# ScalarE as a second row fetcher in two attention stages, and the linear part of an elu on VectorE

## The reference

```python
x = x + gnn(layernorm(x), edges)
x = x + ffn(layernorm(x))

# gnn: one GCN layer (64 wide), two attention layers (4 heads of 64)
h = relu(segment_sum(h[src] * norm[:, None], dst, n) + b)      # GCN, then batch norm
# an attention layer
h = (x @ W).reshape(n, 4, 64)
e = leaky_relu(alpha_s[src] + alpha_d[dst])                    # one logit per edge and head
w = exp(e - emax[dst])
out = segment_sum((w / wsum[dst])[:, :, None] * h[src], dst, n) + b
h = elu(batch_norm(out))
```

## Time and profile before

| | |
|---|---|
| median of three runs | 8129.97 us |
| the profiled execution | 8128.7 us, its span 8126.9 us |
| busy over the span | PE 4740 us (58%), VectorE 4679 (58%), ScalarE 1679 (21%), GpSimd 5035 (62%) |
| GCN edge stage | about 355 to 2375 us |
| attention edge stages | about 2476 to 4557 and 4754 to 6831 us |
| input of the second attention layer | 4557 to 4750 us, its elu 4631 to 4733 |
| the expert part and the rest | 6831 us to the end |

### The profile page before, as it was taken

One profiled execution on the slowest core, in us unless ns is written; L12 is line 12 of the kernel. 1 busy time (PEld: TensorE's weight loads), 2 busy tenths in 40 slices (PEclk: granted clock), 3 DMA queues, 4 the chain that ended last, 5 costly groups with the idle time before them and its releaser, 6 DMA issues. The chain is left out here.

```text
span 8126.9 us, 152076 instructions
## 1 busy us (share of the span) xinstructions
PE 4740.2 (58%) x25092; PEld 3771.0 (46%) x25110; DVE 4678.9 (58%) x11632; ACT 1678.8 (21%) x7056; POOL 5035.3 (62%) x5320
## 2 busy tenths in 40 slices
PE   3444444444454666666656756565665556779994
PEld 3433333333343444444444544444444444559993
DVE  7722222222237777777777767777677777764445
ACT  3400000000022111111111431111111112563331
POOL 0177777777755777777777247777777774015552
PEclk9999999999997777877777787778787876869997
DMA  5411111111124555555555245555555553412226
GB/s 203 162 29 29 29 29 29 29 29 29 29 56 132 137 137 137 137 137 138 136 134 139 69 121 138 137 137 137 137 137 138 137 137 85 140 51 70 70 70 219
DMA packets 527200, 848.14 MB, mean 104 GB/s; under 512 B 147632, under 2 KB 373137, under 8 KB 519791
## 3 DMA queue, kind: packets, MB, share of 16 engines
q0 software_dynamic: 228576, 543.07, 26.7%
q1 hardware_dynamic: 265512, 274.99, 11.7%
q10 hardware_dynamic: 32358, 23.60, 0.9%
HBM read 750.78 MB, written 82.11 MB: 102 GB/s over the span
## 5 line engine op out<-in xcount | busy, mean ns | idle before, releaser
L769 POOL DMA_INDIRECT gat_rows<-gat_table,gat_idx x3278 | 3103.4, 947 | 1057.8 <-issue 944.7
L890 PE MATMUL gat_ps_sum<-gat_msg,gat_hot 128*128 128x260 f32 x6656 | 2267.8, 500 | 1263.5 <-DVE feat L909 1261.0
L890 PEld LDWEIGHTS gat_ps_sum<-gat_msg,gat_hot 128*128 128x128 f32 x6656 | 1562.4, 246 | 1605.0 <-DVE gat_msg L945 1150.5
L769 POOL DMA_INDIRECT gcn_rows<-gcn_table,gcn_idx x1614 | 1523.0, 944 | 787.4 <-issue 478.3
L890 PE MATMUL gcn_ps_sum<-gcn_rows,gcn_hot 128*128 128x64 f32 x3328 | 814.1, 426 | 1228.2 <-DMA gcn_rows<-gcn_table,gcn_idx 724.7
L890 PEld LDWEIGHTS gcn_ps_sum<-gcn_rows,gcn_hot 128*128 128x128 f32 x3328 | 741.1, 328 | 1301.2 <-DMA gcn_rows<-gcn_table,gcn_idx 658.3
L909 DVE SCALAR_TENSOR_TENSOR feat<-gcn_ps_sum,in_first,feat 128x64 f32 x416 | 118.0, 284 | 1572.2 <-PE gcn_ps_sum L890 1572.2
L873 PEld LDWEIGHTS gat_ps_near<-gat_tab,gat_hot_t 128*128 128x128 bf16 x6656 | 268.3, 101 | 766.4 <-issue 579.2
L945 DVE TENSOR_TENSOR gat_msg<-gat_rows,gat_ps_as 128x1024 f32<-128x1024 f32 x416 | 503.2, 1210 | 118.1 <-issue 117.4
L921 DVE TENSOR_TENSOR gat_hot<-gat_count,mod_t 128x512 f32<-128x512 f32 x832 | 566.4, 681 | 2.7
L873 PE MATMUL gat_ps_near<-gat_tab,gat_hot_t 128*128 128x24 bf16 x6656 | 309.8, 178 | 435.4 <-DVE gat_hot L921 431.3
(11 more groups left out here) (308 smaller groups left out, 6375.5 us busy)
## 6 DMA issues: line engine op xcount, KB each, us to landing
gat_mod<-mod_rows SPq DMA_DIRECT2D x832, 128.0 KB
gat_ahead<-gat_table SPq DMA_DIRECT2D x6400, 1.0 KB
gi_mods<-mod_rows SPq DMA_DIRECT2D x52, 1024.0 KB, 4.7
gat_rows<-gat_table,gat_idx POOLq DMA_INDIRECT x3278
gcn_ahead<-gcn_table SPq DMA_DIRECT2D x3200, 0.2 KB
gcn_ahead<-gcn_table ACTq DMA_DIRECT2D x3200, 0.2 KB
gcn_rows<-gcn_table,gcn_idx POOLq DMA_INDIRECT x1614, 2.4
gat_table<-feat SPq DMA_DIRECT2D x28, 910.0 KB, 5.3
```

What stands on the lines that cost most here:

```text
L769: pool.indirect_dma_start(B["rows"][:, j, k, :], None, table, bass.IndirectOffsetOnAxis(ap=B["idx"][:, j, k:k + 1], axis=0)).then_inc(rows ...
L890: mm = pe.matmul(B["ps_sum"][b][:, 0:width], B["hot"][:, j, k, :], rhs, start=(k == 0), stop=(k == CH - 1))
```

## The change

- The helpers of each kind of stage are listed as (period, first group): `HELPERS = {False: ((16, 2), (16, 9)), True: ((16, 2), (16, 9))}`. Attention stages (`True`) thus get the helper on ScalarE that the GCN stage has. GpSimd issues three gathers instead of four for the groups 25, 41, ... to 409, 25 groups per stage.
- ScalarE's program in an attention stage becomes push, weigh, stage, bring, fetch, with a loop of 32 turns instead of 16. Its push comes four turns ahead of the group that it serves (`lead` 4), in the GCN stage one.
- `landed` and `ahead` count for any period; consumers of a chunk wait for `pushed` of the helper that brought it.
- `pace` gets `spare`: the loop stops earlier, so that more of the last turns are unrolled. SyncE's and ScalarE's helper programs use it.
- In the elu, `straight` on ScalarE is removed and VectorE's `line` makes y into the same buffer, one block ahead of `clip` and `unite`.

```diff
-AHEAD = 16
-ATS = (2, 9)
-BURST = P // AHEAD
+HELPERS = {False: ((16, 2), (16, 9)), True: ((16, 2), (16, 9))}
...
-def pace(eng, n, steps, ring=2):
+def pace(eng, n, steps, ring=2, spare=0):
...
-    last = (n - max(leads)) // ring
+    last = (n - max(leads) - spare) // ring
...
-    helpers = 1 if gat else 2
+    helpers = len(HELPERS[gat])
...
-    def ahead(i, c):
+    def ahead(turn, i, c):
 
-        if isinstance(i, int) and AHEAD * i + c < AHEAD:
-            return []
-        return [h for h, at in enumerate(ats) if c % AHEAD == at]
+        return [(h, 16 * (turn // period) * i + 16 * ((c - at) // period)) for h, (period, at) in enumerate(helpers)
+                if c % period == at and not (isinstance(i, int) and turn * i + c < period)]
...
-            for k in range(CH - len(ahead(i, c))):
+            for k in range(CH - len(ahead(TURN, i, c))):
...
-    def helper(eng, h):
+    def helper(eng, h, lead=1):
...
-            if c % AHEAD == at - 1 and known(n):
+            if c % period == at - lead and known(n):
...
-        if gat:
-            pace(act, NG, [(weigh, 2), (stage, RING + 2)], AHEAD)
-        else:
-            bring, fetch, push = helper(act, 1)
-            pace(act, NG, [(push, -AHEAD), (stage, RING), (bring, AHEAD), (fetch, 0)], 2 * AHEAD)
+        bring, fetch, push = helper(act, 1, 4 if gat else 1)
+        steps = [(weigh, 2), (stage, RING + 2)] if gat else [(stage, RING)]
+        pace(act, NG, [(push, -period)] + steps + [(bring, period), (fetch, 0)], turn,
+             period + helpers[1][1])
...
                 def line(q):
-                    if q >= SLOTS:
+                    to = shf if elu else stage
+                    if elu:
+                        wait(dve, staged, q - (SLOTS - 1))
+                    elif q >= SLOTS:
                         dve.wait_ge(product, last(q - SLOTS))
                     for k in range(KP):
-                        ins = dve.tensor_scalar(some(stage, q, k), feat[0:KF, four(q), k * P:(k + 1) * P],
+                        ins = dve.tensor_scalar(some(to, q, k), feat[0:KF, four(q), k * P:(k + 1) * P],
                                                 scale[0:KF, k:k + 1], shift[0:KF, k:k + 1], ALU.mult, ALU.add)
                     ins.then_inc(shifted, 1)
...
-                turns(NQ, [(clip, 0), (unite, 0)] if elu else [(line, 0)])
+                turns(NQ, [(clip, 0), (line, 1), (unite, 0)] if elu else [(line, 0)])
...
-                def straight(q):
-                    wait(act, staged, q - (SLOTS - 1))
-                    for k in range(KP):
-                        ins = act.activation(some(shf, q, k), feat[:, four(q), k * P:(k + 1) * P], ACT.Identity,
-                                             scale=scale[:, k:k + 1], bias=shift[:, k:k + 1])
-                    ins.then_inc(shifted, 1)
...
-                turns(NQ, ([(expo, 2), (straight, 2)] if elu else []) + [(place, 0)])
+                turns(NQ, ([(expo, 2)] if elu else []) + [(place, 0)])
```

More of the change, by code:

```diff
@@ L741, in fast_edges, with landed @@
     rows_used = msg_made if gat else summed
[L742 to L754, removed]
-    def ahead(i, c):
-        if isinstance(i, int) and AHEAD * i + c < AHEAD:
-            return []
-        return [h for h, at in enumerate(ats) if c % AHEAD == at]
+    helpers = HELPERS[gat]
+    TURN = max(period for period, _ in helpers)
+    pushed = [M.sem(f"{L}pushed{h}") for h in range(len(helpers))]
+    ahead_free = [M.sem(f"{L}ahead_free{h}") for h in range(len(helpers))]
+    idx_in = [[M.sem(f"{L}ahead_idx_in{h}{b}") for b in range(2)] for h in range(len(helpers))]
+    ahead_in = [[M.sem(f"{L}ahead_in{h}{b}") for b in range(2)] for h in range(len(helpers))]
+    def landed(turn, i, c):
+        each, rest = CH * turn // RING, CH * (c // RING + 1)
+        for period, at in helpers:
+            if c % RING == at % RING and not (isinstance(i, int) and turn * i + c < period + at):
+                each, rest = each - turn // period, rest - (c - at) // period
+        return 16 * each * i + 16 * rest
+    def ahead(turn, i, c):
+        return [(h, 16 * (turn // period) * i + 16 * ((c - at) // period)) for h, (period, at) in enumerate(helpers)
+                if c % period == at and not (isinstance(i, int) and turn * i + c < period)]
     def gather(pool):
         def group(i, c):
-            j, g = c % RING, AHEAD * i + c
+            j, g = c % RING, TURN * i + c
             pool.wait_ge(idx_staged, g + 1)
@@ L771, in group @@
                                         ).then_inc(rows_in[j], 16)
-        pace(pool, NG, [(group, 0)], AHEAD)
-    def helper(eng, h):
-        at, own = ats[h], ats[h] % RING
-        regs = [eng.alloc_register(f"{L}row{h}_{r}") for r in range(BURST)]
-        count = (NG - 1 - at) // AHEAD
+        pace(pool, NG, [(group, 0)], TURN)
+    def helper(eng, h, lead=1):
+        period, at = helpers[h]
+        own, burst = at % RING, P // period
+        regs = [eng.alloc_register(f"{L}row{h}_{r}") for r in range(burst)]
+        count = (NG - 1 - at) // period
         def known(n):
@@ L799, in fetch @@
                 eng.sem_inc(ahead_free[h], 1)
[L800 removed]
+                eng.wait_ge(idx_in[h][b], 16 * (i + c // period // 2 + 1))
                 eng.sem_inc(ahead_free[h], 1)
[L802 to L804 removed]
+            eng.load(regs, B["ahead_idx"][0:1, h, b, part * burst:(part + 1) * burst])
+            for r in range(burst):
+                p = part * burst + r
                 row = eng.snap(regs[r], min_val=0, max_val=S.N - 1)
@@ L825, in mods @@
                          ).then_inc(mod_in[j], 16)
-        pace(sp, NG, ([(mods, 0)] if gat else []) + [(bring, AHEAD), (fetch, 0), (push, -AHEAD)], 2 * AHEAD)
+        period = helpers[0][0]
+        pace(sp, NG, ([(mods, 0)] if gat else []) + [(bring, period), (fetch, 0), (push, -period)], 2 * period,
+             period + helpers[0][1])
     def act_program(act):
         regs = [act.alloc_register(f"{L}act_w{j}") for j in range(RING)]
-        per = 1 if gat else 2
+        period = helpers[1][0]
+        turn = 2 * period
         def stage(i, c):
-            j, g = c % RING, per * AHEAD * i + c
+            j, g = c % RING, turn * i + c
             used = c - RING
-            wait(act, rows_in[j], landed(per * i, used))
-            for h in ahead(per * i, used):
-                wait(act, pushed[h], 16 * (per * i + used // AHEAD))
+            wait(act, rows_in[j], landed(turn, i, used))
+            for h, count in ahead(turn, i, used):
+                wait(act, pushed[h], count)
             act.copy(B["idx"][:, j, :], at1(K["src_t"], g)).then_inc(idx_staged, 1)
@@ L883, in total @@
                 pe.wait_ge(hot_built, g + 1)
-                pe.wait_ge(rows_in[j], landed(i, c))
-                for h in ahead(i, c):
-                    pe.wait_ge(pushed[h], 16 * (i + c // AHEAD))
+                pe.wait_ge(rows_in[j], landed(TURN, i, c))
+                for h, count in ahead(TURN, i, c):
+                    pe.wait_ge(pushed[h], count)
             wait(pe, added, g - 1)
@@ L931, in logits @@
                                    AX, ALU.add))
-            dve.wait_ge(rows_in[j], landed(i, c))
-            for h in ahead(i, c):
-                dve.wait_ge(pushed[h], 16 * (i + c // AHEAD))
+            dve.wait_ge(rows_in[j], landed(TURN, i, c))
+            for h, count in ahead(TURN, i, c):
+                dve.wait_ge(pushed[h], count)
             link(dve.tensor_tensor(logit, B["rows"][:, j, :, FEAT:ROW], near[:, :, 0:HEADS], ALU.add))
```

36 lines of the change are left out of this document (18 added, 18 removed).

## The result

The changed kernel takes 8211.14 us (median of four runs, 8210.43 to 8212.99) against 8129.67 before: ratio 1.0100, 95% interval 1.0087 to 1.0113. It is slower by 81 us, and 8210 had been forecast. The profiled execution has a span of 8208.7 us, 81.8 more than before.

A forecast was written before the change was run, and what follows sets the result against it. SyncE's and GpSimd's issuing shared the pace; with the fetch ScalarE's would set it. Net 44 us per attention stage, 88 for both, less 8 for the elu: 8128.7 + 80 + 1.3 = 8210 us, range 8095 to 8290.

The forecast's parts named there:

- main step: Attention stages: ScalarE becomes the slowest queue, about 81 us per 16 groups against 79.9 (SyncE) and 77.5 (GpSimd); chance 0.63.
- ScalarE's turn, 4.92 us: Attention stages, per group: old work 0.635, to first row 0.90, eight row DMAs 3.21, back 0.17; 400 turns 1968 us.
- The push: ScalarE, every 16 turns: from the rows' end to the copy 0.99 us instead of 0.17, so +0.82.
- the bring: ScalarE's load of the next 128 numbers: first row 1.50 us behind the copy instead of 0.90, so +0.60.
- the jump: End of ScalarE's 32-turn loop, eight times per stage: 2.8 us each above the normal step, 22 us.
- The end of a stage, -10 us: Behind the 403rd exp: GpSimd being ahead, the stage ends 56 instead of 66 us later; bounds 0 and 10.
- the chains add: Rival: VectorE's way from exp to logits lengthens, ScalarE also waits each turn; 0.2 us of waiting is 160 us: 8370; chance 0.07.
- SyncE's 79.9 us per 16 groups: Attention stages: SyncE's issuing keeps this time, so GpSimd's saved gathers count 0 mid-stage, out of up to 31 us per stage.
- One sign that the prediction named: Attention stages, if the forecast is right: SyncE waits for VectorE's one-hot matrices; no size given.
- The elu, -8: Elu stage: a block of four windows goes from 3.90 to 3.56 us, 24.5 blocks, 8 us saved; bounds 0 and 10.
- 8098 to 8258: Forecast times in us from the bounds of ScalarE's turn alone, 4.78 and 4.98 us.
- +54: Middle of each attention stage, third to 403rd exp: 2026 us instead of 1971.7, a loss of 54 us.

The follow-up runs named there:

- the two-instruction run: The kernel whose fetched chunk nobody reads, with two semaphore increments added in VectorE's program ahead of the second attention stage's loop: 8209.5 us, ratio 1.0097.
- the kernel that throws the chunk away: The changed kernel, but ScalarE's fetched rows are pushed to a spare tile nobody reads and GpSimd gathers 63 chunks of 64 as before: 8190.2 us, ratio 1.0073.

## Why the prediction was right

Its main step, that ScalarE becomes the longest queue, was right and is shown: the same fetch with cheaper issue (unrolled, or half the issues) lets the 100 us go. Term by term:

- *ScalarE's turn, 4.92 us.* In the loop of the first stage the 243 turns without push, load of numbers or jump take 4.93 us on average. Two of the pieces are off and cancel: exp to second copy 0.80 (forecast 0.635), from there to the first row 0.78 (0.90), the eight rows 3.18 (3.21), rows' end to exp 0.17 (0.17). The mean over all turns of the loop, pushes and jumps included, is 5.09 us in the first stage, forecast as 2026 / 400 = 5.07. The push cost 0.75 (forecast 0.82), the bring 0.65 (0.60), the jump about 3.4 (2.8).
- *What was mis-sized there:* the prediction took all 400 turns as turns of the loop. The 64 before it and the 48 behind it are straight code, with a mean of 4.82 and 4.71 us. That makes the first stage's middle 2000.0 instead of 2026.
- *The end of a stage, -10 us.* Measured -2.0 and -3.4. GpSimd did draw ahead of ScalarE in the loop, as the prediction had it. But in the 48 straight turns behind the loop ScalarE, at 4.71 us a turn or 75 us per 16, was faster than GpSimd with 62 gathers of 1.25 us (77.5), and the lead was used up before the 403rd exp. Order of time, changed kernel, first gather and exp of the 301st group, then of the 401st:

```profile
3997.34 0.95 POOL L767 DMA_INDIRECT gat_rows<-gat_table,gat_idx  x1 [0.30 <-issue]
...
4014.39 0.19 ACT L858 ACTIVATE gat_ps_rel<-gat_logit 128x16 f32<-128x16 f32 x1 [3.82 <-issue]
...
4495.00 0.95 POOL L767 DMA_INDIRECT gat_rows<-gat_table,gat_idx  x1 [0.30 <-issue]
...
4503.21 0.19 ACT L858 ACTIVATE gat_ps_rel<-gat_logit 128x16 f32<-128x16 f32 x1 [3.59 <-DVE gat_logit L939]
```

  The lead is 17.1 us for the one and 8.2 for the other, in the kernel before 10.9 and 8.5. So what was booked for the end had come back within the middle.
- *The jump that no term had.* VectorE's loop stalls 4.3 us per 16 groups in the second stage and ScalarE waits for it, worth about 19 us by the two-instruction run. The prediction's rival "the chains add" came in that way, in one turn of 16 only. ScalarE's own second stop in that stage had no term either.
- *SyncE and GpSimd.* That the saved gathers are worth little beside ScalarE's pace is shown by the kernel that throws the chunk away: 5 us in the first stage, where 31 are saved. That they count in full when no other queue is in the way is shown too. SyncE's 79.9 us per 16 groups is, like ScalarE's 5.07, a figure of its loop: in the kernel with ScalarE's issues halved its loop takes 159.1 us per 32 in the first stage, but 16 groups of the middle 78.1 on average, since SyncE's straight code is faster (75 us per 16 near the end). One sign that the prediction named is missing: SyncE hardly waits for VectorE's one-hot matrices, 1.3 us in 5 waits between 2600 and 4400, as before. It waits at its push, for messages (38.7 us in 14, before 9.4 in 4).
- *The elu, -8.* Measured -6.6 in its stage; a block takes 3.56 us as forecast. Order of time, ScalarE:

```profile
4669.65 1.50 ACT L1510 ACTIVATE gat_in_ex<-feat,gat_in_shift,gat_in_scale 128x512 f32<-128x512 f32 x2
...
4673.21 1.50 ACT L1510 ACTIVATE gat_in_ex<-feat,gat_in_shift,gat_in_scale 128x512 f32<-128x512 f32 x2
```

What was missed is the same edit's effect further on, in the loops of the second attention stage.

So 8210 against 8211 is closer than the working deserved. Of the prediction's two ranges for this case, 8098 to 8258 comes from the turn's bounds and 8146 to 8290 is not worked out. The prediction had +54 - 10 for each stage: 88, less 8 for the elu. Measured are +26.3 and +60.0, less 6.6. An overestimate in the straight code and stalls that it did not know cancelled; that part of the agreement is luck. The remaining part of the second stage's excess over the first (33.7 us, of which the run shows 19) was not tried. In the trace it lies in the turn behind ScalarE's jump, 7.46 us there and 5.71 in the first stage, and the second stop of ScalarE in that turn, 14 us in all, is about its size.

The rule of the Trainium skill (Runtime: NRT & Kernel Launch, Instruction fetch mechanics) that the prediction cited holds for ScalarE's attention loop as well, with 3.65 us at the jump above. The eight jumps of the first stage's loop cost some 27 us (forecast 22), which a forecast without that stall, 8166, leaves out.

## What to carry to other kernels

Before giving a queue that looks idle more DMAs to issue, add up its whole turn in issue time and set it beside the longest queue's; with 5.09 us per group in the loop against 4.93 before (1971.7 / 400) the time rose by 81 us, and with the same issues written out straight it fell by 25. Unroll or thin out the issues (half of SyncE's rows to let ScalarE's in) so that the engine that was relieved becomes the bound again, or the relief is worth nothing. When two kernels differ by a few instructions, look at the jumps of each engine's loop in both before explaining a difference by the edit. And do not take a turn in a loop for a turn in straight code: here they were 5.09 and 4.7 to 4.8 us.

## What the runs showed of the hardware

- Two instructions more or less ahead of a loop can decide whether its jump costs anything. VectorE's loop of 337 instructions took 0.23 us from branch to next instruction in one place and 4.25 us two semaphore increments later. In the kernel before it was 3.2 in both stages, in the changed one 3.3 and 4.3. The loops of GpSimd (100 instructions) jump in 0.1 to 0.2 us everywhere. The Trainium skill (Runtime: NRT & Kernel Launch, Instruction fetch mechanics) says that a taken branch to a page out of the window waits for its fetch. The runs agree, and add that the place can matter more than the length. Which places are good was not mapped. What a jump costs depends on what it holds up: on ScalarE it was paid in full between DMA issues (3.65 us at the jump above) and mostly hidden behind queued copies (0.71 us idle).
- A single-row DMA issue with its address in a register comes every 0.38 us on ScalarE (median; eight take 3.12 us, first to last). A second row in the same DMA costs its queue little: with two rows an issue comes every 0.41 us, and from the load to the end of the issues ScalarE took 2.59 us with four of two rows (median of a turn) and 4.01 with eight of one.
- SyncE's and ScalarE's issues side by side did not slow each other: SyncE's rows came every 0.42 us in both kernels.
